# Self attention of a fused decoder layer: both maximum pairs of a key tile move between its second score matmul and the weighing, and the loop over groups is written out

## The reference, cut to what matters

```
scores = jnp.einsum('bhqd,bhkd->bhqk', q, k) / np.float32(np.sqrt(hd))
scale = jax.nn.sigmoid(jnp.einsum('bhsd,hd->bhs', q, scale_w)) * 2.0
scores = scores * scale[..., None]
aw = jax.nn.softmax(scores, axis=-1)
out = jnp.einsum('bhqk,bhkd->bhqd', aw, v).transpose(0, 2, 1, 3).reshape(b, s, d)
```

## Time and profile before

| | |
|---|---|
| median of 3 runs | 2220.33 us (2219.41 to 2221.75) |
| the profiled execution | 2223.34 us, its span 2221.6 us |
| self attention in it | about 387 to 1160 us from the span's start |
| TensorE busy, whole span | 1745.5 us (79%) |
| VectorE busy | 1333.2 us (60%), of them 604.6 in the 512 maxima (line 988) |
| ScalarE busy | 947.5 us (43%), of them 530.0 in the 1024 exponentials (line 1071) |
| mean granted clock of TensorE | 0.882 |

### The profile page before, as it was taken

One profiled execution on the slowest core, in us unless ns is written; L12 is line 12 of the kernel. 1 busy time (PEld: TensorE's weight loads), 2 busy tenths in 40 slices (PEclk: granted clock), 3 DMA queues, 4 the chain that ended last, 5 costly groups with the idle time before them and its releaser, 6 DMA issues. The chain is left out here.

```text
span 2221.6 us, 32909 instructions
## 1 busy us (share of the span) xinstructions
PE 1745.5 (79%) x10156; PEld 811.2 (37%) x10157; DVE 1333.2 (60%) x2309; ACT 947.5 (43%) x1700; POOL 504.1 (23%) x529
## 2 busy tenths in 40 slices
PE   5899696699999999999996841998068995015997
PEld 3466463122222222222224630676044652012654
DVE  5344253888888888788832540665783544793221
ACT  3323274277777777677772310443242322001110
POOL 4200043700000000000002425333760002056343
PEclk9899898699999999999997865999589998556998
DMA  4000078411122111131004016121200004201352
GB/s 128 1 2 1 25 258 272 97 35 36 36 49 55 35 35 35 36 66 38 2 1 164 0 39 233 55 66 57 73 1 1 2 1 153 84 0 39 95 133 29
DMA packets 114348, 137.07 MB, mean 62 GB/s; under 512 B 16545, under 2 KB 90401, under 8 KB 113953
## 3 DMA queue, kind: packets, MB, share of 16 engines
q1 hardware_dynamic: 99376, 113.34, 18.5%
q0 software_dynamic: 9216, 16.79, 3.3%
q10 hardware_dynamic: 5616, 5.11, 0.7%
HBM read 78.31 MB, written 56.89 MB: 61 GB/s over the span
## 5 line engine op out<-in xcount | busy, mean ns | idle before, releaser
L988 DVE TENSOR_REDUCE sa_mhalf<-sa_a 128x2 f32<-128x1024 f32 x512 | 604.6, 1218 | 69.1 <-PE sa_a L1093 66.9
L1071 ACT ACTIVATE sa_e<-sa_b 128x512 f32<-128x512 f32 x1024 | 530.0, 602 | 234.3 <-PE sa_b L1120 234.0
L1120 PE MATMUL sa_b<-sa_q,sa_k 112*128 112x512 bf16 x1024 | 315.0, 389 | 11.9 <-issue 8.1
L1130 PE MATMUL sa_ops<-sa_e,sa_v 128*17 128x512 f32 x2048 | 272.8, 605 | 0.7 <-ACT sa_e L1071 0.7
L1093 PE MATMUL sa_a<-sa_k,sa_q 48*128 48x512 bf16 x1024 | 207.7, 403 | 42.1 <-DMA sa_k<-k_parts 24.6
L1240 POOL TENSOR_TENSOR ao_var<-ao_mv,x_eps_pow 128x4 f32<-128x4 f32 x8 | 1.6, 201 | 805.7 <-DVE ao_mv L1339 805.7
L1093 PEld LDWEIGHTS sa_a<-sa_k,sa_q 48*128 48x128 bf16 x1024 | 49.4, 93 | 330.3 <-issue 196.1
L1120 PEld LDWEIGHTS sa_b<-sa_q,sa_k 112*128 112x128 bf16 x1024 | 78.1, 97 | 168.6 <-issue 85.1
L213 DVE TENSOR_REDUCE xa_mx<-xa_rows 128x16 f32<-128x1024 f32 x64 | 78.3, 1223 | 100.1 <-PE xa_rows L445 100.1
L360 ACT ACTIVATE xa_pT<-xa_cols 128x1024 f32<-128x1024 f32 x64 | 62.0, 1021 | 84.7 <-PE xa_cols L477 84.7
L2521 DVE TENSOR_TENSOR sw_hT<-sw_p,sw_act 128x512 f32<-128x512 f32 x32 | 22.1, 691 | 108.6 <-PE sw_p L2466 105.9
(11 more groups left out here) (327 smaller groups left out, 2778.2 us busy)
## 6 DMA issues: line engine op xcount, KB each, us to landing
k_parts<-sp_kpart SPq DMA_DIRECT2D x96, 128.0 KB, 1.8
sa_q<-q_parts SPq DMA_DIRECT2D x64, 192.0 KB, 5.1
sa_k<-k_parts SPq DMA_DIRECT2D x64, 192.0 KB, 5.6
tc_w<-in_L_ffn_W SPq DMA_DIRECT2D x24, 512.0 KB
q_parts<-sp_qpart SPq DMA_DIRECT2D x16, 384.0 KB, 3.2
expert_in<-ao_zero SPq DMA_DIRECT2D x1, 4992.0 KB, 23.0
expert_out<-ex_xb ACTq DMA_DIRECT2D x39, 128.0 KB, 1.7
v_groups<-sp_vt SPq DMA_DIRECT2D x8, 544.0 KB, 4.0
```

Of the source, the lines that this page charges most:

```text
L988: nc.vector.tensor_reduce(mhalf[par][:, half, head:head + PAIRED + 1:PAIRED, t], aps[at][:], axis=X, op=ALU.max).then_inc(a_used, 1)
L1071: nc.scalar.activation(ex[kt % 2][:, head], bps[(2 * (2 * s + qc) + i) % 3][:], ACT.Exp, scale=SCALE).then_inc(exp_done, 1)
L1120: nc.tensor.matmul(bps[(2 * (2 * s + qc) + i) % 3][:], ks[s][:, head, kt * P:(kt + 1) * P], qs[s][:, head, qc * CW:(qc + 1) * CW], start=T ...
L1130: last = nc.tensor.matmul(ops[32 * head:32 * head + VW], vs[s][:, kt, head], ex[kt % 2][:, head], start=(kt == 0), stop=(kt == KT - 1))
```

## The change

TensorE's key tile becomes S0, S1, F, F, W, (transpose), S2, S3. VectorE's reads follow: in key tiles 2 and 4 both maxima come ahead of `split_max` and `normalize`. The numbers of the uses shift by one where a transpose now comes after the second pair (`max_use`, `out_use`). ScalarE's `keep_out` moves from behind the third exponential of a unit to behind its second. `groups` writes out all 16 groups on all engines; no waits against registers are left, and helpers that asked whether a number is known when the program is built are gone. The banks, tiles and their numbers stay: three `bps`, two `aps`.

```diff
     def max_use(a):
-        if isinstance(a, int) and a == 0:
+        if a == 0:
             return TILE_MAXIMA
-        if isinstance(a, int) and a == UNITS - 1:
+        if a == UNITS - 1:
             return first_use(a - 1) + 4
-        return first_use(a - 1) + 5
+        return first_use(a - 1) + 6
 
     def out_use(n):
...
-        return first_use(n) + 10
+        return first_use(n) + 11
...
-        def groups(eng, body):
-
-            body(0, 0, 0, 0, 1)
-            with eng.Fori(0, GROUPS // SETS - 1) as i:
-                for j in range(1, 1 + SETS):
-                    body(i * SETS + j, i + j // SETS, j % SETS, i + (j + 1) // SETS, (j + 1) % SETS)
-            for g in range(GROUPS - SETS, GROUPS):
+        def groups(body):
+
+            for g in range(GROUPS):
                 body(g, g // SETS, g % SETS, (g + 1) // SETS, (g + 1) % SETS)
...
                         for kt in range(KT):
-                            if kt == 2 and not (isinstance(n, int) and n + 1 >= UNITS):
+                            if kt == 2 and n + 1 < UNITS:
                                 combine(n + 1, (qc + 1) % 2, base + offset)
                             for which in range(2):
-                                if which == 1 and kt == 2 and not (isinstance(n, int) and n + 1 >= UNITS):
-                                    split_max(n + 1, base + offset, at(offset))
-                                    offset += 1
-                                if which == 1 and kt == 4:
-                                    normalize(n, base + offset, at(offset))
-                                    offset += 1
                                 if ahead(n, kt, which):
                                     a, k = ahead(n, kt, which)
-                                    maximum((qc + (1 if kt < 2 else 0)) % 2, k, base + offset, at(offset))
+                                    maximum((qc + (1 if kt < 2 else 0)) % 2, k, base + offset, (base + offset) % 2)
                                     offset += 1
+                            if kt == 2 and n + 1 < UNITS:
+                                split_max(n + 1, base + offset, (base + offset) % 2)
+                                offset += 1
+                            if kt == 4:
+                                normalize(n, base + offset, (base + offset) % 2)
+                                offset += 1
...
-                            if i == 2 and later(n, 1):
+                            if i == 1 and n >= 1:
                                 keep_out(n)
...
                         for kt in range(KT):
-                            for head in range(GH):
+                            for head in range(2):
                                 scores(n, GH * kt + head, s, turn, qc)
-                                if head == 2:
-                                    if kt:
-                                        weigh_values(n, kt - 1, s, turn)
-                                    elif qc:
-                                        weigh_values(n - 1, KT - 1, s, turn)
-                                    elif later(g, 1):
-                                        weigh_values(n - 1, KT - 1, (s - 1) % SETS, turn)
-                                if head == 2 and kt == 2 and not (isinstance(n, int) and n + 1 >= UNITS):
-                                    transpose_max(n + 1, base + offset, at(offset))
+                            for which in range(2):
+                                if ahead(n, kt, which):
+                                    a, k = ahead(n, kt, which)
+                                    if kt < 2 and qc == 0:
+                                        first_scores(k, base + offset, (base + offset) % 2, s, turn, 1)
+                                    else:
+                                        first_scores(k, base + offset, (base + offset) % 2, s1, turn1, 0 if kt < 2 else qc)
                                     offset += 1
-                                if head == 2 and kt == 4:
-                                    transpose_out(n, base + offset, at(offset))
-                                    offset += 1
-                                if head in (0, 2) and ahead(n, kt, head // 2):
-                                    a, k = ahead(n, kt, head // 2)
-                                    if kt < 2 and qc == 0:
-                                        first_scores(k, base + offset, at(offset), s, turn, 1)
-                                    else:
-                                        first_scores(k, base + offset, at(offset), s1, turn1, 0 if kt < 2 else qc)
-                                    offset += 1
+                            if kt:
+                                weigh_values(n, kt - 1, s, turn)
+                            elif qc:
+                                weigh_values(n - 1, KT - 1, s, turn)
+                            elif g >= 1:
+                                weigh_values(n - 1, KT - 1, (s - 1) % SETS, turn)
+                            if kt == 2 and n + 1 < UNITS:
+                                transpose_max(n + 1, base + offset, (base + offset) % 2)
+                                offset += 1
+                            if kt == 4:
+                                transpose_out(n, base + offset, (base + offset) % 2)
+                                offset += 1
+                            for head in range(2, GH):
+                                scores(n, GH * kt + head, s, turn, qc)
```

More of the change, by code:

```diff
@@ L863, in first_use @@
     def first_use(n):
-        if isinstance(n, int) and n >= UNITS - 1:
+        if n >= UNITS - 1:
             return FIRST + USES * (UNITS - 2) + 6 + n - (UNITS - 1)
@@ L868, in max_use @@
     def max_use(a):
-        if isinstance(a, int) and a == 0:
+        if a == 0:
             return TILE_MAXIMA
-        if isinstance(a, int) and a == UNITS - 1:
+        if a == UNITS - 1:
             return first_use(a - 1) + 4
-        return first_use(a - 1) + 5
+        return first_use(a - 1) + 6
     def out_use(n):
-        if isinstance(n, int) and n >= UNITS - 2:
+        if n >= UNITS - 2:
             return first_use(n) + (5 if n == UNITS - 2 else 0)
-        return first_use(n) + 10
+        return first_use(n) + 11
     with ExitStack() as ctx:
@@ L917, in ahead @@
             a, k = (n + 1, EARLY + 2 * kt + which) if kt < 2 else (n + 2, 2 * (kt - 2) + which)
-            return None if isinstance(a, int) and a >= UNITS else (a, k)
+            return None if a >= UNITS else (a, k)
         with nc.Block() as block:
@@ L949, in body @@
                 def body(g, turn, s, turn1, s1):
-                    if not (isinstance(g, int) and g + 2 >= GROUPS):
-                        if later(g, 1):
+                    if g + 2 < GROUPS:
+                        if g >= 1:
                             sp.wait_ge(pv_done, 2 * KT * g)
-                        load(g + 2, (s + 2) % SETS, isinstance(g, int) and g == 0)
+                        load(g + 2, (s + 2) % SETS, g == 0)
                     pass_max(2 * g + 1, s, 1)
-                    if not (isinstance(g, int) and g + 1 >= GROUPS):
+                    if g + 1 < GROUPS:
                         pass_max(2 * g + 2, s1, 0)
@@ L961, in _ @@
                 pass_max(0, 0, 0)
-                groups(sp, body)
+                groups(body)
             @block.gpsimd
@@ L999, in split_max @@
                     dve.wait_ge(a_filled, use + 1)
-                    if later(a, 1):
+                    if a >= 1:
                         dve.wait_ge(m_stored, 16 * a)
@@ L1051, in _ @@
                     maximum(1, k, TILE_MAXIMA + 1 + k, (TILE_MAXIMA + 1 + k) % 2)
-                groups(dve, body)
+                groups(body)
                 normalize(UNITS, out_use(UNITS), out_use(UNITS) % 2)
@@ L1067, in body @@
                             kt, head = i // GH, i % GH
-                            if head == 0 and later(n, 1) or kt >= 2 and head == 0:
+                            if head == 0 and n >= 1 or kt >= 2 and head == 0:
                                 act.wait_ge(pv_done, KT * n + kt - 1)
@@ L1072, in body @@
                                                  scale=SCALE).then_inc(exp_done, 1)
-                            if i == 2 and later(n, 1):
+                            if i == 1 and n >= 1:
                                 keep_out(n)
                 act.wait_ge(out_cleared, 2)
-                groups(act, body)
+                groups(body)
                 keep_out(UNITS)
@@ L1082, in fill @@
                 def fill(use):
-                    if later(use, 2):
+                    if use >= 2:
                         pe.wait_ge(a_used, use - 1)
@@ L1103, in transpose_out @@
                 def transpose_out(n, use, at):
-                    if later(n, 1):
+                    if n >= 1:
                         pe.wait_ge(o_evacuated, n)
@@ L1117, in scores @@
                         pe.wait_ge(m_loaded, 32 * (n + 1))
```

(4 more changed lines are left out.)

4 lines of the change are left out of this document (removed).

## The result

| | before | after |
|---|---|---|
| median | 2219.87 us (2218.96 to 2221.75, 4 runs) | 2265.82 us (2260.11 to 2271.17, 4 runs) |
| profiled execution, span | 2221.6 us | 2265.3 us |
| 30 intervals of `combine` | 696.0 us | 742.5 us |

The ratio is 1.0205 (95% interval 1.0179 to 1.0232): 46 us slower, where 41.4 were forecast, in the range and by the mechanism that the prediction named. The four runs of the changed kernel lie 0.5% apart from end to end; so do 13 runs of the kernel before, taken beside the last experiments (2215.76 to 2225.65), and the width says nothing of the change. In the two traces the span grew by 43.7 us and the last `combine` came 42.65 us later (1129.92 to 1172.57), so nearly all of the loss lies in self attention.

The account below looks back on a forecast made before the run. TensorE's queue was taken to set the pace in self attention. A unit of 8 x 2.92 + 1.02 + 0.20 = 24.58 us, 30 times, gives 737.4 against 696.0: +41.4, so 2261.5 us; range 2245 to 2281.

Parts of the forecast that it names:

- the mechanism that the prediction named: In self attention, four score matmuls in a row on three banks make the fourth wait for the first one's exponential.
- The wait on the bank: In TensorE's row of four scores, the fourth starts 1.08 us after the first, held until an exponential frees its bank.
- F to F at 0.22: On TensorE, the second maximum pair starts 0.22 us after the first, estimated from the lower clock; bounds 0.21 and 0.32.
- The key tile of 2.92: TensorE's time for one key tile of self attention in the new order: 2.92 us, against 2.71 before.
- The rival with a dear pair: Maximum pair behind maximum pair costs a full change of matmul kind, 0.32 us: 24 us more, 2286 us; chance 5%.
- The count of changes of kind: TensorE's switches between score, maximum and weighing matmuls per key tile: four in place of five, giving back 0.10 us.
- The transposes: At key tiles 2 and 4, transposes wait 0.20 us each for a maxima bank; with what follows, 1.02 us a unit.
- The copy: ScalarE's output copy, moved ahead of the exponential on which the next second score waits: +0.20 us a unit.
- The loop: Writing out the loop over groups removes three back-edge pauses, 14.5 us, and 2.9 us from 24 units; 17.4 together.
- that rival: Fetching the written-out code costs what the back edges cost, so 17.4 us are not gained: 2279 us; chance 7%.
- The faster case: Saved change of matmul kind wins if the fourth score does not wait: key tile 2.57, 43 us less, 2178; chance 10%.
- Start and tail: Unit 0 at the lower clock, and unit 30 from key tile 2, keep their patterns: 0, give or take 1 us.

## Why the prediction was right

- **The wait on the bank**, 1.08 from S2 to S1: measured 1.08. Three experiments bear on it: with three in a row it is gone (key tile 2.60), with shorter exponentials it shrinks by what they do, and with the loop kept it is the same.
- **F to F at 0.22**, the estimate from the lower clock: 0.21. The key tile of 2.92 is exact. The rival with a dear pair is out.
- **The count of changes of kind** in the prediction is wrong, though its sum is not. "One change of kind fewer, four in place of five": S0, S1, F, F, W, S2, S3 has three (S to F, F to W, W to S), two fewer than before. That is why 0.42 lost to the bank and "0.10" given back do not make the 0.21 between 2.71 and 2.92, while 0.42 less 0.20 is 0.22. The sum itself went by starts and holds the right number of each. The size of a change, 0.10 us, is the trace's alone: the Trainium skill's page, "TensorEngine Tiling (Array Packing)", Key Properties, says that changing the mode drains TensorE, but gives no time that could agree "in size".
- **The transposes** were the mis-sized term: "it waits 0.20, twice a unit" is 0.29 each (1.81 - 1.52), because TensorE goes on 0.15 after the maximum and not 0.06. The 0.06 was read between an exponential and a score, where one wait stands ahead of the matmul; a transpose has two. What follows them, 0.12 + 0.50 in the sum, is 0.10 + 0.47. Together 1.15 for 1.02, so 24.70 a unit for 24.58, some 3.5 us over 29 or 30 units.
- **The copy**, 0.20 a unit: 0.19 in the trace. The step blames the new place; but put back behind the third exponential the copy costs as much, by way of W.
- **The loop**, 17.4: 17.5 by the intervals, and 19 by the medians. No pause appears in the written-out code, so that rival is out too. The prediction took the 14.5 us for pauses alone; a part of it was the lower clock behind them.
- **The faster case** forecast a key tile of 2.57, by two changes of kind saved. The run with S2 moved saves one (four in place of five) and has 2.60 where 2.71 stood, so what a saved change gives back is real, 0.11 here. What kept the changed order from its gain was the fourth score in a row on a ring of three banks. Whether VectorE's two tiles would have held it at 2.57 no run shows.
- **Start and tail**, "0, give or take 1": the first two intervals are 20.33 and 26.29 where 22.07 and 22.91 stood, so 1.7 us moved from the first, which the 30 leave out, into the second. Of the 46.5 us that the 30 intervals grew, 41.4 were forecast, 1.7 are this shift, and the rest is the transposes. The medians grew by 46, the profiled spans by 43.7; the difference of the two is not explained, but is within the spread of the runs.

## What to carry to other kernels

Count how many producers of one ring stand in a row in the queue, not how many per round: with three banks the fourth waits for the full latency of its first consumer (start, length and release, here 1.08 us), however idle that consumer is, unless other work of that length stands between. Before work is moved out from between them, ask which latency it covered; here one score put ahead of the weighing, and the copy back in its place, turned 46 us lost into 34 won, 19 of which are the loop's. And undo steps one at a time: a wait that is removed at one instruction may be paid at the next one, as the copy shows.

## What the runs showed that was not expected

- In this kernel a transpose with two waits ahead of it goes on about 0.15 us after the later one, if that is the one kept in an instruction of its own, and 0.06 if the transpose itself carries it; swapping two lines saved 0.155 us a unit.
- In the loop the transposes start 0.06 after the maximum and not 0.15, twice a unit; on the other side the fourth score behind the copy comes 0.09 later than written out (1.36 behind the first of the row in place of 1.27). That is why its unit (24.64) is shorter than the written-out one (24.70). That the 0.09 is the arithmetic of the waits against registers is likely, but not shown.
- The same three back edges cost 14.5 us with the old order and 9.8 with the new one, though TensorE idles 8.1 and 8.2 us at them. The rest goes with the granted clock, which fell behind all three pauses in the old order and behind two in the new.
